# The residual additions of the last stage on VectorE instead of GpSimd, and seven tiles of sums on VectorE instead of five

## The chip, the core and the metric

One core of a Trainium2 chip runs the whole program. The metric is the device time of one execution in microseconds. The engines are called PE (TensorE), DVE (VectorE), ACT (ScalarE), POOL (GpSimd) and SP (SyncE, which here issues transfers and waits).

## What is computed

The reference is one transformer layer with post-normalised branches: attention over 4 x 512 tokens of width 512, then a mixture of 64 experts of which each token uses 8, plus a shared expert.

```python
x = x + _layernorm(_L0_attn_ref(_layernorm(x), Wq, Wk, Wv, Wo))
x = x + _layernorm(_L0_ffn_ref(_layernorm(x), router_w, Wg, Wu, Wd, Wsg, Wsu, Wsd, Wse))

# _L0_ffn_ref: top 8 of 64 experts, weights normalised to sum 1
routed = sum over e of comb[:, e] * ((silu(xt @ wg_e.T) * (xt @ wu_e.T)) @ wd_e.T)
shared = sigmoid(xt @ Wse.T) * ((silu(xt @ Wsg.T) * (xt @ Wsu.T)) @ Wsd.T)
return routed + shared
```

The change touches only the last line of this: the sum `routed + shared`, its layer normalisation, and the addition to `x`.

## The kernel before

The 2048 tokens are 16 tiles of 128 rows (TILES). Attention runs first, then the router and the shared expert, then a loop over some 158 tiles of gathered rows for the experts. Each expert tile's result is added by POOL's indirect DMA into one of three tables in HBM (`sum_rows`, 3 x 2048 x 512, TABLES = 3); the first table starts from the shared expert's output, the others from zero. When the last of these writes has landed, POOL raises `s_routed`, and the last stage begins, written out by hand and without a loop in the machine code.

The last stage, for the 16 tiles in order:

- **SP** waits for `s_routed` and issues 16 loads (L369), 768 KB each: for tile i the three partial sums of its 128 tokens, 128 x 3 x 512, into `sums_of(i)`. These lie in the storage of earlier stages, so the profile calls them `big` (tiles 0 to 7), `x_t` (8 to 11) and `attn_t` (12 to 15). Behind the loads SP issues the 16 outputs (L375), 256 KB each, in order, each once its tile's last addition is done (`s_fin` from POOL, `s_fin_dve` from DVE).
- **PE** sums the three parts of the tiles in `SUM_ON_PE` by three matmuls with the identity matrix into a PSUM bank (L1021); the trace shows each matmul as two instructions. Before, these are tiles 0, 1, 3, 4, 6, 7, 9, 10, 12, 13 and 15. Four banks take turns.
- **DVE** sums the other five tiles (2, 5, 8, 11, 14) by two additions (L1353, L1354). For every tile it takes the statistics (L1359, from PSUM or from SBUF) and aggregates them to mean and variance (L1360). One step later, for tile i - 1, it inverts the deviation (L1364) and forms the bias as a product of mean and inverse (L1365, 128x1). `step(...)` makes the next instruction of DVE wait for the end of this one.
- **ACT** takes the square root for tile i (L695), then normalises tile i - 1 with scale and bias (L700) back into `sums_of(i - 1)[:, 0, :]` and raises `s_norm`.
- **POOL** adds the normalised tile to `x_sb` (L526, the residual) for 14 tiles; DVE does it for tiles 13 and 15 behind all its other work (L1370).

What the engines wait for is set by semaphores: DVE for `s_sums[i]` (a load) or `s_sum_ps` (PE), for `s_lnf` (ACT's square root) before L1364, and for `s_norm` before a residual; ACT for `s_lnb` and `s_lnd` from DVE; PE for `s_sums[i]`, and from its fifth tile on for `s_norm` of the tile that had the bank before.

Of the kernel before, what the change touches and what calls it, by code (L numbers as in the profile page):

```python
# [11 lines left out]
ALU = mybir.AluOpType  # L12
# [9 lines left out]
TILES = B * TB  # L22
# [27 lines left out]
FIRST_STEPS = [("xt", 0), ("xt", 1), ("proj", 0), ("xt", 2), ("proj", 1), ("xt", 3), ("proj", 2), ("qkt", 0),  # L50
               ("proj", 3), ("qkt", 1)]

LAST_ON_DVE = (TILES - 3, TILES - 1)
NOWHERE = TABLES * B * S
SUM_ON_PE = tuple(i for i in range(TILES) if i % 3 != 2)
LAST_ON_POOL = tuple(i for i in range(TILES) if i not in LAST_ON_DVE)

NORM_X_AT = (BLOCKS - 6, BLOCKS - 5, BLOCKS - 3, BLOCKS - 2)

# [1 line left out]
def sandwich_kernel(nc, x, wqkv, wo, router, experts, rope, mask, ident, before, ones, upto, below,  # L61
                    steps, count, token, out):
    ctx = ExitStack()
    with ctx:
        def sb(name, shape, dtype=FP32):
            return ctx.enter_context(nc.sbuf_tensor(name, shape, dtype))

        def sem(name):
            return ctx.enter_context(nc.semaphore(name))


        x_sb = sb("x_sb", [P, TILES, D])
# [88 lines left out]
        def sums_of(i):  # L161
            return sums[i // TB][:, i % TB, :, :]
# [120 lines left out]
        s_lnd = sem("s_lnd")  # L283
        s_norm = sem("s_norm")
        s_fin = sem("s_fin")
        s_fin_dve = sem("s_fin_dve")
        s_out = sem("s_out")
        s_x2d = [sem(f"s_x2d{p}") for p in range(2)]
        s_combd = sem("s_combd")
# [7 lines left out]
        def sum_bank(i):  # L297
            return ps[:, 4 + SUM_ON_PE.index(i) % 4, :]

# [22 lines left out]
        def _(sp):  # L322
# [45 lines left out]
            for i in range(TILES):  # L368
                sp.dma_start(sums_of(i), all_sums_v[:, i, :, :]).then_inc(s_sums[i], 16)  # L369
            for i in range(TILES):  # L370
                if i in LAST_ON_POOL:
                    sp.wait_ge(s_fin, LAST_ON_POOL.index(i) + 1)
                else:
                    sp.wait_ge(s_fin_dve, LAST_ON_DVE.index(i) + 1)
                sp.dma_start(out_v[:, i, :], x_sb[:, i, :]).then_inc(s_out, 16)  # L375
            sp.wait_ge(s_out, 16 * TILES)

# [1 line left out]
        def _(pool):  # L379
# [45 lines left out]
            for i in range(TILES + 4):  # L425
                if i < TILES:
                    pool.wait_ge(s_stat, i + 1)
                    pool.tensor_tensor(out=x_sb[:, i, :], in0=x_sb[:, i, :], in1=delta[:, i % 2, :],
                                       op=ALU.add).then_inc(s_x1, 1)
                if i == 0:  # L430
                    pool.memset(earlier[:, 0, :], 0.0).then_inc(s_first, 1)
                if i >= 4:
                    k = i - 4
# [3 lines left out]
                    else:  # L437
                        pool.wait_ge(s_prefix, k)
                    pool.tensor_tensor(out=earlier[:, k + 1, :], in0=earlier[:, k, :], in1=chosen[:, k, :],
                                       op=ALU.add).then_inc(s_prefix, 1)  # L440

            for i in range(TILES):
                pool.wait_ge(s_up, i + 1)
                if i >= 2:
                    pool.wait_ge(s_sht, i - 1)
                pool.tensor_tensor(out=hidden[:, i % 2, :], in0=gate[:, i % 2, :], in1=up_s[:, i % 2, :],
                                   op=ALU.mult).then_inc(s_shid, 1)
# [72 lines left out]
                pool.wait_ge(s_scatter[p], (full * 2 + (5 if p == 0 else 4)) * 16)  # L520
                pool.sem_inc(s_issue, 1)
            pool.sem_inc(s_routed, 1)

            for i in LAST_ON_POOL:
                pool.wait_ge(s_norm, i + 1)
                pool.tensor_tensor(out=x_sb[:, i, :], in0=x_sb[:, i, :], in1=sums_of(i)[:, 0, :],  # L526
                                   op=ALU.add).then_inc(s_fin, 1)

        @block.scalar
        def _(act):  # L530
# [161 lines left out]
            for i in range(TILES + 1):  # L692
# [3 lines left out]
                if i >= 1:  # L696
                    k = i - 1
                    act.wait_ge(s_lnd, k + 1)
                    total = sum_bank(k) if k in SUM_ON_PE else sums_of(k)[:, 0, :]
                    act.activation(sums_of(k)[:, 0, :], total, ACT.Identity, bias=moments[:, k, 0:1],  # L700
# [3 lines left out]
        def _(pe):  # L704
# [310 lines left out]

            for n, i in enumerate(SUM_ON_PE):
                pe.wait_ge(s_sums[i], 16)
                if n >= 4:
                    pe.wait_ge(s_norm, SUM_ON_PE[n - 4] + 1)
                for p in range(TABLES):  # L1020
# [4 lines left out]
        def _(dve):  # L1025
# [118 lines left out]
            def step(ins):  # L1144

                own[0] += 1
                ins.then_inc(s_own, 1)
                dve.wait_ge(s_own, own[0])
# [7 lines left out]
            for i in range(TILES + 4):  # L1156
                y_in, x_in, l_in = i < TILES, 1 <= i <= TILES, i >= 4
                r, k = i - 1, i - 4
# [73 lines left out]
            for half in range(2):  # L1232
                dve.wait_ge(s_slots_ps, half + 1)
                dve.scalar_tensor_tensor(out=slots[:, 8 * half:8 * half + 8, :],
                                         in0=ps[:, half, :].rearrange("p (t e) -> p t e", e=E), scalar=1.0,
                                         in1=chosen[:, 8 * half:8 * half + 8, :], op0=ALU.add,
# [30 lines left out]
            for m in range(TILES * K):  # L1267
                t, k = divmod(m, K)
# [78 lines left out]
            def total_of(i):  # L1347
                if i in SUM_ON_PE:
                    dve.wait_ge(s_sum_ps, SUM_ON_PE.index(i) + 1)
                    return sum_bank(i)  # L1350
                y = sums_of(i)[:, 0, :]
                dve.wait_ge(s_sums[i], 16)
                step(dve.tensor_tensor(out=y, in0=y, in1=sums_of(i)[:, 1, :], op=ALU.add))  # L1353
                step(dve.tensor_tensor(out=y, in0=y, in1=sums_of(i)[:, 2, :], op=ALU.add))  # L1354
                return y

            for i in range(TILES + 1):
                if i < TILES:
                    step(dve.bn_stats(stats[:, i, :], total_of(i)))  # L1359
                    dve.bn_aggr(moments[:, i, :], stats[:, i, :]).then_inc(s_lnb, 1)  # L1360
                if i >= 1:
                    k = i - 1
                    dve.wait_ge(s_lnf, k + 1)
                    step(dve.reciprocal(rstd[:, k:k + 1], rstd[:, k:k + 1]))  # L1364
                    dve.scalar_tensor_tensor(out=moments[:, k, 0:1], in0=moments[:, k, 0:1], scalar=-1.0,  # L1365
                                             in1=rstd[:, k:k + 1], op0=ALU.mult, op1=ALU.mult).then_inc(s_lnd, 1)

            for i in LAST_ON_DVE:
                dve.wait_ge(s_norm, i + 1)
                dve.tensor_tensor(out=x_sb[:, i, :], in0=x_sb[:, i, :], in1=sums_of(i)[:, 0, :],  # L1370
                                  op=ALU.add).then_inc(s_fin_dve, 1)


def _constants():
# [55 lines left out]
```

## Time and profile before

| | us |
|---|---|
| median of 3 runs | 1173.39 |
| lowest, highest | 1172.31, 1174.42 |
| the profiled execution, in all | 1172.27 |
| its span, first to last instruction | 1170.4 |
| busy PE / DVE / ACT / POOL | 1074.4 / 670.3 / 505.3 / 630.5 |
| first load of the last stage issued | 1115.44 |
| last residual addition ends | 1165.60 |

The profile is of one execution. Times in it count from the first instruction. A row of the timeline gives start, duration, engine, line, operation, the tiles written and read, and in brackets how long the engine had been idle and who released it; several equal instructions in a row are merged. The chain of waits is followed back from the last instruction: at each step to what released it. Matmuls are pipelined and their ends are modelled, and spans on POOL are rough. The granted clock of PE has two levels, 1.00 (2.4 GHz) and 0.50 (1.2 GHz).

### The profile page before, as it was taken

Reading aid. Unit: us, or ns where it says so; the run is one execution under the profiler, and the core shown is the slowest. Engines: PE = TensorE matmul, PEld = TensorE weight load, DVE = VectorE, ACT = ScalarE, POOL = GpSimd, SP = SyncE. Lnnn points to the kernel's source line nnn. Section 1 sums busy time; section 2 is a strip of 40 time slices with the busy share of each in tenths; the row PEclk is TensorE's granted clock in tenths of the full one; section 3 lists DMA queues with packets and bytes.
Section 4 is the critical chain, followed back from the end, with each engine's and each line's share of the span. In section 5 each row is a group of like instructions: output and inputs, shape, how many; then the busy total and the mean of one; then the engine's idle time right before and its main releaser. Section 6 shows DMA issues by size and latency. Waiting matters only on the chain.

```text
span 1170.4 us, 24429 instructions
## 1 busy us (share of the span) xinstructions
PE 1074.4 (92%) x6281; PEld 724.3 (62%) x6282; DVE 670.3 (57%) x2288; ACT 505.3 (43%) x1421; POOL 630.5 (54%) x648
## 2 busy tenths in 40 slices
PE   5999899899999979988869999999999999999973
PEld 3555566555566546555547777777777777677621
DVE  5666566556666668867635544544444444454447
ACT  2666566566666644436622222222222222222223
POOL 3433333433333313321148788887888888788824
PEclk9999999999999999989989999999999999999987
DMA  9700000000000052100169999999999999997796
GB/s 316 288 2 1 3 1 1 2 2 1 1 2 2 1 196 84 63 19 19 66 198 213 219 215 251 236 237 238 256 231 251 243 228 277 258 230 151 114 326 252
DMA packets 66279, 166.73 MB, mean 142 GB/s; under 512 B 15378, under 2 KB 17170, under 8 KB 66080
## 3 DMA queue, kind: packets, MB, share of 16 engines
q0 software_dynamic: 38496, 83.95, 32.5%
q1 hardware_dynamic: 27712, 81.88, 19.9%
q8 instruction: 39, 0.64, 0.2%
q14 instruction: 32, 0.26, 0.1%
HBM read 119.85 MB, written 62.65 MB: 156 GB/s over the span
## 4 chain that ended last, share of the span: by engine, by line
PE 66%; DMA 18%; DVE 6%; issue 5%; ACT 2%; POOL 2%; POOLq 0%; DVEq 0%; SPq 0%; ACTq 0%
PE ps L721 15%; PE ps L982 12%; DMA sum_rows<-x_t,idx 11%; PE ps L780 6%; PE ps L993 6%; DMA x_t<-x_rows,idx 5%; PE ps L838 4%; PE ps L750 4%; PE ps L800 4%; PE ps L966 3%; PE ps L874 2%; PE ps L735 2%; PE ps L890 2%; PE ps L854 1%; POOL x_t L464 1%
## 5 line engine op out<-in xcount | busy, mean ns | idle before, releaser
L982 PE MATMUL ps<-big,work 128*128 x1264 | 300.1, 380 | 0.0
L470 POOL DMA_INDIRECT sum_rows<-x_t,idx x157 | 249.9, 1592 | 53.8 <-issue 40.2
L982 PEld LDWEIGHTS ps<-big,work 128*128 128x128 f32 x1264 | 228.7, 191 | 24.8
L464 POOL DMA_INDIRECT x_t<-x_rows,idx x159 | 166.3, 1046 | 58.9 <-issue 29.0
L721 PE MATMUL ps<-big 128*128 128x384 f32 x512 | 180.1, 495 | 2.1 <-ACT big L539 1.7
L390 POOL TENSOR_TENSOR work<-qkv_all,rope_sb 128x256 f32<-128x256 f32 x64 | 46.8, 731 | 243.6 <-ACT qkv_all L544 243.6
L675 ACT ACTIVATE work<-ps 128x512 f32<-128x512 f32 x159 | 95.0, 597 | 185.4 <-PE ps L966 114.2
L993 PE MATMUL ps<-big,work 128*128 x314 | 160.9, 594 | 0.6 <-issue 0.5
L966 PEld LDWEIGHTS ps<-ident_sb,x_t 128*128 128x128 f32 x636 | 78.3, 142 | 105.9 <-issue 71.9
L1087 DVE CUSTOM_DVE_ANT_0 ps<-ps,mask_sb 128x128 f32<-128x128 f32 (+3 forms) x256 | 120.5, 512 | 24.1 <-PE ps L750 23.4
L563 ACT ACTIVATE work<-ps,neg_max 128x128 f32<-128x128 f32 (+3 forms) x256 | 132.5, 528 | 3.3 <-DVE neg_max L1087 2.2
L721 PEld LDWEIGHTS ps<-big 128*128 128x128 f32 x512 | 94.3, 194 | 56.9 <-issue 4.0
L1311 DVE SCALAR_TENSOR_TENSOR work<-work,small,ps 128x128 f32<-128x128 f32 x157 | 54.5, 347 | 128.5 <-ACT work L680 93.4
L680 ACT ACTIVATE work<-ps 128x128 f32<-128x128 f32 x157 | 43.6, 278 | 195.7 <-PE ps L982 141.8
L569 ACT ACTIVATE x_t<-ps 128x128 f32<-128x128 f32 (+2 forms) x192 | 77.0, 436 | 90.5 <-PE ps L780 90.5
L966 PE MATMUL ps<-ident_sb,x_t 128*128 128x128 f32 x636 | 97.5, 276 | 17.7 <-DMA x_t<-x_rows,idx 15.8
L780 PE MATMUL ps<-ident_sb,work 128*128 128x128 f32 x640 | 98.6, 285 | 9.1 <-issue 6.0
L1319 DVE TENSOR_SCALAR x_t<-ps 128x512 f32<-128x512 f32 x157 | 106.8, 681 | 0.0
L780 PEld LDWEIGHTS ps<-ident_sb,work 128*128 128x128 f32 x640 | 69.0, 142 | 46.1 <-issue 35.1
L1108 DVE TENSOR_TENSOR attn_t<-ps,work 128x128 f32 (+1 forms) x64 | 18.6, 291 | 110.2 <-PE ps L800 110.2
L1305 DVE TENSOR_SCALAR small<-x_t 128x1 f32 x158 | 24.3, 154 | 76.1 <-issue 72.3
L993 PEld LDWEIGHTS ps<-big,work 128*128 128x128 f32 x314 | 59.1, 190 | 10.7 <-issue 3.0
(184 smaller groups left out, 1471.7 us busy)
## 6 DMA issues: line engine op xcount, KB each, us to landing
big<-experts SPq DMA_DIRECT2D x65, 768.0 KB, 14.4
sum_rows<-x_t POOLq DMA_DIRECT2D x4, 2048.0 KB
big<-sum_rows SPq DMA_DIRECT2D x8, 768.0 KB, 9.6
x_rows<-work SPq DMA_DIRECT2D x16, 256.0 KB, 2.0
sum_rows<-attn_t POOLq DMA_DIRECT2D x2, 2048.0 KB
out<-x_sb SPq DMA_DIRECT2D x16, 256.0 KB, 6.1
x_sb<-x SPq DMA_DIRECT2D x3, 1024.0 KB, 10.5
x_t<-sum_rows SPq DMA_DIRECT2D x4, 768.0 KB, 13.1
```

The costliest lines, as they stand in the source:

```text
L464: pool.indirect_dma_start(rows[:, q, :], None, x2_rows, bass.IndirectOffsetOnAxis(ap=idx[:, q, 0:1], axis=0), bounds_check=last_row, oob_i ...
L470: pool.indirect_dma_start(all_sums, bass.IndirectOffsetOnAxis(ap=idx[:, q, 1:2], axis=0), y_sb[:, q, :], None, bounds_check=last_sum, oob_ ...
L563: act.activation(probs[:, h, 0:n], s_bank[h][:, 0:n], ACT.Exp, bias=neg_max[:, h:h + 1], scale=-1.0, accum_out=den[:, h:h + 1]).then_inc(s ...
L569: act.activation(probs_t[:, i % 2, h, 0:qt + 1, :], pt_bank[h % 2].rearrange("p (k n) -> p k n", k=TB)[:, 0:qt + 1, :], ACT.Copy).then_inc ...
L675: act.activation(rows_t[:, p, :, :], ps[:, p, :].rearrange("p (c n) -> p c n", c=DC), ACT.Copy).then_inc(s_xg, 1)
L721: mm = pe.matmul(bank[:, 0:QKV], x_t[:, c, bass.ts(t, P)], wqkv_sb[:, c, g % G, :], start=(c == 0), stop=(c == DC - 1))
L780: mm = pe.transpose(pt_bank[h % 2][:, bass.ts(c, P)], probs[:, h, bass.ts(c, P)], ident_sb[:, :])
L966: mm = pe.transpose(ps[:, p, bass.ts(c, P)], rows[:, q, bass.ts(c, P)], ident_sb[:, :])
L982: mm = pe.matmul(ps[:, 2 + p, 0:GATEUP], rows_t[:, p, c, :], w_ring[:, slot, c * GATEUP:(c + 1) * GATEUP], start=(c == 0), stop=(c == DC - 1))
L993: pe.matmul(ps[:, 5 + p, :], hidden_t[:, p, :], w_ring[:, slot, DC * GATEUP:WCOLS], start=True, stop=True).then_inc(s_dn, 1)
L1087: dve.tensor_tensor_reduce(sc, sc, mask_sb[:, S - n:S], -SCALE, 3.0e38, ALU.add, ALU.min, neg_max[:, h:h + 1]).then_inc(s_masked, 1)
L1319: dve.tensor_scalar(y_sb[:, q, :], ps[:, 5 + q % 2, :], 1.0, None, ALU.mult).then_inc(s_y, 1)
```

## The change

POOL's loop of residual additions goes, with `LAST_ON_POOL`, `LAST_ON_DVE` and `s_fin_dve`. DVE adds the residual of every tile within its loop, three steps behind the statistics, and the loop is two steps longer. `SUM_ON_PE` becomes tiles 1, 2, 4, 6, 7, 9, 11, 12 and 14; DVE sums tiles 0, 3, 5, 8, 10, 13 and 15. SP waits for one semaphore.

```diff
-LAST_ON_DVE = (TILES - 3, TILES - 1)
-SUM_ON_PE = tuple(i for i in range(TILES) if i % 3 != 2)
-LAST_ON_POOL = tuple(i for i in range(TILES) if i not in LAST_ON_DVE)
+SUM_ON_PE = tuple(i for i in range(TILES) if i not in (0, 3, 5, 8, 10, 13, 15))
...
             for i in range(TILES):
-                if i in LAST_ON_POOL:
-                    sp.wait_ge(s_fin, LAST_ON_POOL.index(i) + 1)
-                else:
-                    sp.wait_ge(s_fin_dve, LAST_ON_DVE.index(i) + 1)
+                sp.wait_ge(s_fin, i + 1)
                 sp.dma_start(out_v[:, i, :], x_sb[:, i, :]).then_inc(s_out, 16)
...
-            for i in LAST_ON_POOL:
-                pool.wait_ge(s_norm, i + 1)
-                pool.tensor_tensor(out=x_sb[:, i, :], in0=x_sb[:, i, :], in1=sums_of(i)[:, 0, :],
-                                   op=ALU.add).then_inc(s_fin, 1)
...
-            for i in range(TILES + 1):
+            for i in range(TILES + 3):
                 if i < TILES:
                     step(dve.bn_stats(stats[:, i, :], total_of(i)))
                     dve.bn_aggr(moments[:, i, :], stats[:, i, :]).then_inc(s_lnb, 1)
-                if i >= 1:
+                if 1 <= i <= TILES:
                     k = i - 1
...
-            for i in LAST_ON_DVE:
-                dve.wait_ge(s_norm, i + 1)
-                dve.tensor_tensor(out=x_sb[:, i, :], in0=x_sb[:, i, :], in1=sums_of(i)[:, 0, :],
-                                  op=ALU.add).then_inc(s_fin_dve, 1)
+                if i >= 3:
+                    k = i - 3
+                    dve.wait_ge(s_norm, k + 1)
+                    dve.tensor_tensor(out=x_sb[:, k, :], in0=x_sb[:, k, :], in1=sums_of(k)[:, 0, :],
+                                      op=ALU.add).then_inc(s_fin, 1)
```

How it moves the instructions of DVE. At the start of the last stage, behind the last copy of the expert loop, before:

```order
L1319 TENSOR_SCALAR x_t<-ps 128x512
L1359 BN_STATS stats<-ps 128x6
L1360 BN_AGGR moments<-stats 128x2
L1359 BN_STATS stats<-ps 128x6
L1360 BN_AGGR moments<-stats 128x2
L1364 RECIPROCAL rstd<-rstd 128x1
L1365 SCALAR_TENSOR_TENSOR moments<-moments,rstd 128x1
L1353 TENSOR_TENSOR big<-big 128x512
L1354 TENSOR_TENSOR big<-big 128x512
L1359 BN_STATS stats<-big 128x6
```

and in the changed kernel (where the lines are 11 lower: 1342 and 1343 are the two additions, 1348 and 1349 the statistics, 1353 and 1354 the factors):

```order
L1308 TENSOR_SCALAR x_t<-ps 128x512
L1342 TENSOR_TENSOR big<-big 128x512
L1343 TENSOR_TENSOR big<-big 128x512
L1348 BN_STATS stats<-big 128x6
L1349 BN_AGGR moments<-stats 128x2
L1348 BN_STATS stats<-ps 128x6
L1349 BN_AGGR moments<-stats 128x2
L1353 RECIPROCAL rstd<-rstd 128x1
L1354 SCALAR_TENSOR_TENSOR moments<-moments,rstd 128x1
L1348 BN_STATS stats<-ps 128x6
L1349 BN_AGGR moments<-stats 128x2
```

Tile 0 is now summed by DVE ahead of everything, and the first two tiles that need PE are 1 and 2. At the end of the stage on DVE, before, from the additions of tile 14 on:

```order
L1353 TENSOR_TENSOR attn_t<-attn_t 128x512
L1354 TENSOR_TENSOR attn_t<-attn_t 128x512
L1359 BN_STATS stats<-attn_t 128x6
L1360 BN_AGGR moments<-stats 128x2
L1364 RECIPROCAL rstd<-rstd 128x1
L1365 SCALAR_TENSOR_TENSOR moments<-moments,rstd 128x1
L1359 BN_STATS stats<-ps 128x6
L1360 BN_AGGR moments<-stats 128x2
L1364 RECIPROCAL rstd<-rstd 128x1
L1365 SCALAR_TENSOR_TENSOR moments<-moments,rstd 128x1
L1364 RECIPROCAL rstd<-rstd 128x1
L1365 SCALAR_TENSOR_TENSOR moments<-moments,rstd 128x1
```

and now, from the residual of tile 11 and the additions of tile 15 on:

```order
L1359 TENSOR_TENSOR x_sb<-x_sb,x_t 128x512
L1342 TENSOR_TENSOR attn_t<-attn_t 128x512
L1343 TENSOR_TENSOR attn_t<-attn_t 128x512
L1348 BN_STATS stats<-attn_t 128x6
L1349 BN_AGGR moments<-stats 128x2
L1353 RECIPROCAL rstd<-rstd 128x1
L1354 SCALAR_TENSOR_TENSOR moments<-moments,rstd 128x1
L1359 TENSOR_TENSOR x_sb<-x_sb,attn_t 128x512
L1353 RECIPROCAL rstd<-rstd 128x1
L1354 SCALAR_TENSOR_TENSOR moments<-moments,rstd 128x1
L1359 TENSOR_TENSOR x_sb<-x_sb,attn_t 128x512 x3
```

The residuals (now L1359) stand between the steps, one per tile, and three remain behind the last factors; the two additions of the last tile, 15, are DVE's own. On POOL the last stage's 14 additions are gone and nothing stands in their place:

```order
L513 ISA x2
L520 ISA
L526 TENSOR_TENSOR x_sb<-x_sb,big 128x512 x8
L526 TENSOR_TENSOR x_sb<-x_sb,x_t 128x512 x4
L526 TENSOR_TENSOR x_sb<-x_sb,attn_t 128x512 x2
```

is what POOL had before behind its last indirect DMA; the changed program ends there with the three waiting instructions.

## Rows read from the trace of the kernel before

**Rows 1.** Busy time by stretch; count in brackets; last clock, DMA share, GB/s.
```profile
core 0: us, PE busy (x) PEld busy (x) DVE busy (x) ACT busy (x) POOL busy (x), PEclk, DMA share, GB/s
1120.00:1130.00 10.00, 10.00 (x20) 4.51 (x21) 3.72 (x9) 1.31 (x3) 0.92 (x1) 0.84 1.05 388
...
1140.00:1150.00 10.00, 8.79 (x21) 3.52 (x19) 9.66 (x20) 4.68 (x9) 5.50 (x5) 1.00 1.05 388
```

**Rows 2.** Chain of waits: start, duration, what; its start and end in this stage.
```profile
1115.44 4.50 DMA big<-sum_rows
1119.98 7.02 PE ps L1021 x12
1127.03 0.71 DVE stats L1359
...
1162.42 0.19 DVE moments L1360
```

**Rows 3.** Timeline of DVE: first tiles, POOL still idle (or starting at 1129.08).
```profile
1124.45 0.70 DVE L1359 BATCH_NORM_STATS2 stats<-ps 128x6 f32<-128x512 f32 x1 [13.91 <-PE ps L1021]
...
1127.03 0.70 DVE L1359 BATCH_NORM_STATS2 stats<-ps 128x6 f32<-128x512 f32 x1 [1.66 <-PE ps L1021]
...
1128.10 0.68 DVE L1353 TENSOR_TENSOR big<-big 128x512 f32<-128x512 f32 x1
...
1128.82 0.69 DVE L1354 TENSOR_TENSOR big<-big 128x512 f32<-128x512 f32 x1
...
1130.62 0.69 DVE L1359 BATCH_NORM_STATS2 stats<-ps 128x6 f32<-128x512 f32 x1
```

**Rows 4.** Timeline and groups of instructions: DVE where POOL adds residuals.
```profile
1131.59 1.26 POOL L526 TENSOR_TENSOR x_sb<-x_sb,big 128x512 f32<-128x512 f32 x1 [0.95 <-ACT big L700]
1131.60 1.26 DVE L1365 SCALAR_TENSOR_TENSOR moments<-moments,rstd 128x1 f32<-128x1 f32 x1
...
1133.79 2.95 POOL L526 TENSOR_TENSOR x_sb<-x_sb,big 128x512 f32<-128x512 f32 x2 [0.94 <-ACT big L700]
1133.85 1.77 DVE L1353 TENSOR_TENSOR big<-big 128x512 f32<-128x512 f32 x1
...
L1365 DVE SCALAR_TENSOR_TENSOR moments<-moments,rstd 128x1 f32<-128x1 f32 x16 | 7.0, 434 | 0.6
L1353 DVE TENSOR_TENSOR x_t<-x_t 128x512 f32<-128x512 f32 x2 | 3.5, 1764 | 0.0
L1354 DVE TENSOR_TENSOR x_t<-x_t 128x512 f32<-128x512 f32 x2 | 3.3, 1636 | 0.1
```

**Rows 5.** Issue and time to landing: second and last of the 16 loads.
```profile
1115.88 0.48 SPq L369 DMA_DIRECT2D big<-sum_rows  x1
big<-sum_rows SPq DMA_DIRECT2D x1, 768.0 KB, 6.0
...
1137.53 1.91 SPq L369 DMA_DIRECT2D attn_t<-sum_rows  x1
attn_t<-sum_rows SPq DMA_DIRECT2D x1, 768.0 KB, 13.3
```

**Rows 6.** Busy time by stretch: PE at its start, and with gaps between tiles.
```profile
1122.50:1123.00 0.50, 0.50 (x2) 0.29 (x1) 0.00 (x0) 0.00 (x0) 0.00 (x0) 0.50 1.04 393
1123.00:1123.50 0.50, 0.50 (x2) 0.15 (x2) 0.00 (x0) 0.00 (x0) 0.00 (x0) 0.78 1.07 410
...
1144.00:1146.00 2.00, 1.16 (x3) 0.68 (x4) 1.93 (x4) 0.00 (x0) 0.52 (x1) 1.00 1.05 387
```

**Rows 7.** Timeline and output issues: the end of the kernel.
```profile
1161.70 0.69 DVE L1359 BATCH_NORM_STATS2 stats<-ps 128x6 f32<-128x512 f32 x1
...
1163.24 0.69 DVE L1370 TENSOR_TENSOR x_sb<-x_sb,attn_t 128x512 f32<-128x512 f32 x1
...
1164.40 1.20 DVE L1370 TENSOR_TENSOR x_sb<-x_sb,attn_t 128x512 f32<-128x512 f32 x1 [0.47 <-ACT attn_t L700]
...
out<-x_sb SPq DMA_DIRECT2D x3, 256.0 KB, 2.0
```

**Rows 8.** Timeline of DVE in the expert loop: two instructions without a wait between.
```profile
1103.47 0.68 DVE L1319 TENSOR_SCALAR x_t<-ps 128x512 f32<-128x512 f32 x1
1104.07 0.28 DVE L1323 TENSOR_SCALAR work<-ps 128x128 f32<-128x128 f32 x1
```

More of the change, by code:

```diff
@@ L285, in sandwich_kernel @@
         s_fin = sem("s_fin")
-        s_fin_dve = sem("s_fin_dve")
         s_out = sem("s_out")
```

## Prediction, made before the changed kernel was run

> **What bounds the kernel now.** The diff touches only the end, from the first load of a sums tile on, so I read that stretch alone. The time by stage [rows 1] shows the rate of the loads and how much POOL has to do beside VectorE; the chain of waits [rows 2] shows which engine sets the end. The loads start at 1115.44, the first lands 4.5 us later, TensorE sums two tiles in its slow clock, and from 1127.03 to 1162.6 every piece of the chain is VectorE; TensorE, ScalarE and the DMA queue are never in it again. So the end is VectorE's own instruction stream plus what holds it up.
>
> Clean cycles [rows 3]. A tile summed on TensorE costs VectorE 1.07 us (statistics at 1127.03, next tile's first instruction at 1128.10). A tile that VectorE sums costs 2.52 (1128.10 to 1130.62): two additions 0.72 apart, then the same cycle.
>
> Cycles with POOL at work [rows 4]. At 1131.59 POOL starts a residual; VectorE's 128x1 product, clean 0.16, starts 10 ns later and takes 1.26, ending with POOL's addition. At 1133.85 a 0.68 addition takes 1.77. L1365 sums to 7.0 us over 16 instructions where 16 x 0.16 is 2.6: 4.4 lost. The first statistics at 1124.45 and the last at 1161.70 [rows 7] are 37.25 apart. Ten TensorE tiles (10.7), five own (12.6) and the slower first tile (2.58 for 1.07, so 1.5) make 24.8. That leaves 12.4. The groups account for it: the 4.4, and for four tiles both additions, 1.77 + 1.64 where 1.37 is clean, 4 x 2.04 = 8.2, together 12.6. It is VectorE standing behind POOL.
>
> The Trainium skill has this ("SBUF — State Buffer", Who interferes with whom): a VectorE instruction with two inputs in SBUF and a GpSimd one that reads SBUF cannot run together, the later waits for the whole of the earlier. The rows agree: 1.26 for 0.16. By that page nothing is blocked once POOL is silent, which is the sum below; if it were false here, rival C.
>
> **What the change removes.** POOL's 14 residuals, and the 12.4 us with them. The other cause of long additions would be the loads into the same memory; at 1128.10 to 1129.5 they run at 0.68 and 0.69 while DMA moves 388 GB/s and POOL has done nothing yet [rows 1, 3]. POOL frees nobody else: it is in no wait but SP's for s_fin.
>
> **What it adds on VectorE.** Sixteen residual additions in the stream (two of them stood at its end before), and two more tiles to sum (seven for five). An uncontended residual takes 0.69 [rows 7]. In the stream it is followed by an instruction that waits for nothing of it, so its price is start to start. The nearest rows are a 0.68 tensor_scalar of the same size and its follower 0.60 later [rows 8]. I take 0.61, the same 0.08 less than its duration; the upper end is 0.72, as L1353 to L1354, if the follower had to wait. Nothing lower is plausible.
>
> The skill speaks against my 0.61 ("VectorE: DVE Perf Modes", The DRAIN you can't avoid): eight copies took the same time with a semaphore after each as with one at the end. By that a residual would cost the 0.72, and the end would be 1.6 later (15 x 0.11). The 0.60 of rows 8 decides for me; it is the second half of rival B.
>
> **The start is a new wait.** Tile 0 goes from TensorE to VectorE. VectorE can begin when it lands at 1119.94 and is through its statistics and aggregation at about 1122.3. TensorE now starts with tile 1, which lands at 1115.88 + 6.0 = 1121.88 [rows 5], 1.94 later than tile 0. Before, TensorE's first tile took 4.47 from start to statistics (1119.98 to 1124.45), as the granted clock was 0.50 (the lower level, 1.2 GHz) after the idle stretch; the half microsecond from 1123.0 shows 0.78, so it rose to 1.00 at about 1123.2, 3.2 behind the first matmul [rows 6]; the second took 2.58. With the same warm-up: statistics of tile 1 at 1124.45 + 1.94 = 1126.39, of tile 2 at 1128.97. So VectorE's four-microsecond head start is spent waiting, then 1.5 more on tile 2. Doing tile 0 there costs and gains nothing on the path, since what follows hangs on TensorE.
>
> **The sum**, from the statistics of tile 2 at 1128.97:
> - tile 2: 1.07; tiles 3, 5, 8, 10, 13 on VectorE: 5 x 2.52 = 12.60; tiles 4, 6, 7, 9, 11, 12, 14: 7 x 1.07 = 7.49.
> - the residuals of tiles 0 to 11, one behind each of tiles 3 to 14: 12 x 0.61 = 7.32. Tile 15 begins at 1157.45.
> - its two additions: 1.45. From its statistics: aggregation, the factors of tile 14, residual 12, the factors of 15 and residuals 13, 14, 15. The pieces are 0.72, 0.10, 0.17, 0.07, 0.61, 0.20, 0.07, 0.61, 0.61 and 0.69 = 3.85. ScalarE's square root and both normalisations (0.29 and 0.8 each) fit beside residuals 12 to 14: the last normalisation is through some 2.95 behind the statistics, the last residual starts at 3.16.
> - end of the last residual: 1157.45 + 1.45 + 3.85 = 1162.75, against 1164.40 + 1.20 = 1165.60 now. **2.85 us earlier.**
>
> Are the inputs there? Loads land every 2.07 us ((1137.53 + 13.3 - 1121.88) / 14, rows 5), the last at 1150.8 for a tile that begins at 1157.45; tile 3 lands at 1126.0 and is wanted at 1130.04. TensorE's tile 4 is ready at 1131.55 and wanted at 1133.2, the least slack, 1.6; tile 14 is ready at 1151.5 and wanted at 1155.8. ScalarE has 1.1 us per tile. A residual stands two tiles behind its factors, so it waits for no normalisation until the last. Behind a waiting residual on VectorE would stand the next tile's additions, and behind those ScalarE and SP.
>
> What follows the last addition stays: the last output is issued right behind it and lands in 2.0 [rows 7]. Outputs 12 to 15 come 0.6 to 0.9 apart, 256 KB each, and at 388 GB/s one takes 0.68, so at most 0.1 us of queueing. The profiled execution is 1172.27 us in all (span 1170.4); less 2.85 is 1169.4. It was 1.12 below the median of the three runs, 1173.39; the forecast for a median is **1170.5 us**, 0.24% less. Of this kernel some 0.2% (2.3 us) can be told from no change.
>
> **Rivals.**
> A. As summed, 1170.5, faster. For: the same arithmetic, with the 12.6 from the groups, closes on the stream before within 0.2 us. With the clock rising during tile 1 instead of near its end, 1.0 less, 1169.5.
>
> B. The gain shrinks under 2.3 us. Either TensorE's clock rises later against its first matmul than the 3.2 us of the profile: all of tile 1 at 0.50 is 2 x 2.58 + 0.2 = 5.4 for 4.47, +0.9; tile 2 partly too, +1.7 (before, the same wait would move with it, so part of this cancels against a median). Or each residual costs 0.72, 15 x 0.11 = +1.6. That gives 1171.4 to 1172.2. The untouched 1115 us may also move by what the three runs spread, 2.1.
>
> C. Slower: the long additions are due to the loads after all, not to POOL. Then the 14 sum additions take 1.7 (+1.0 each, 14.0) and the residuals while loads run (about eight) 1.2 (+0.5 each, 4.0), and the end is 18 later than my sum: 1188. It decides as soon as the 30 additions of the stream take 0.10 longer each than clean (3.0, the gain). Against: the clean pair at 388 GB/s and the 10 ns behind POOL at 1131.60.
>
> D. Slower: TensorE, with nine tiles and gaps of 1 to 2 us between them, stays at or falls to 0.50. A tile is then 5.16; nine end at 1121.9 + 46.4 = 1168.3, and 1.07 + 0.61 + 1.45 + 3.85 behind that is 1175.3, 12.5 over my sum: 1183. From a rise about 9 us after the first matmul on (3.2 + 2 x 2.85) the gain is gone. Against: from 1144 to 1146 TensorE was busy for 58% and the clock stayed 1.00 [rows 6], and in a slow clock the backlog fills the gaps.
>
> E. The gain stays in the queue: the last outputs come faster than they can be written. Were three of them in the queue when the last residual ends, that is 3 x 0.68 = 2.0 more, 1172.5. Against: SP issues outputs from 1139.5 on, behind the last load; by then my sum has residuals 0 to 2 done, and from there they come 1.7 to 3.1 apart.
>
> **Chances.** A 0.58, B and E 0.36 (same), C 0.03, D 0.03 (slower). Faster 0.58, same 0.36, slower 0.06. The range takes in A's early clock with 1.3 of spread (1168.2), and E or B's worst with 0.7 to 1.0 of it (1173.2).
>
> **What would show it.** In the profile after: L1354 (the product) at 0.16 everywhere and both sum additions at 0.68 to 0.69; 16 residuals at 0.69 with 0.61 to the next start; statistics of tile 2 near 4.5 + 2.6 behind TensorE's start; the chain VectorE alone from there for 33.8 us; POOL without busy time. A median above 1173, an addition over 0.8 with POOL idle, or VectorE waiting for TensorE after tile 2 would make the prediction wrong.

## The result, and the profile after

The changed kernel is faster: 1167.32 us median of six runs (1166.20 to 1169.17) against 1173.76 for the kernel before in the same runs, a ratio of 0.9948 (95% interval 0.9936 to 0.9961), 6.4 us. The profiled execution took 1166.61 (span 1164.8) against 1172.27 (span 1170.4), 5.7 us less. The forecast was 2.85 us less and a range that ended at 1168.2: right in its sign, and the size was half of what came. In another set of runs the ratio is 0.9943 (0.9922 to 0.9965), so the gain is not chance.

Where the time went in the two profiles, measured from the issue of the stage's first load:

| us | before | after | forecast for after |
|---|---|---|---|
| first load issued, in the span | 1115.44 | 1115.18 | 1115.44 |
| TensorE's first tile starts | 4.54 behind it | 6.41 | 6.48 |
| statistics of tile 2 | 14.11 | 13.37 | 13.53 |
| last residual ends | 50.16 | 46.97 | 47.31 |
| end of the span behind the last residual | 4.8 | 2.65 | 4.8 |

The last three lines are the case. The stage up to the last residual came as forecast within 0.34 us: 3.2 less where 2.85 was worked out. The rest, 2.15, is behind the last residual, where the prediction said nothing would change. Another 0.26 of the 5.6 between the two spans is the expert loop ahead of the stage.

VectorE's timeline after, at the start and around tiles 2 and 3 (columns as in rows 3; L1342 and L1343 are the two additions, L1348 and L1349 the statistics, L1353 and L1354 the factors, L1359 the residual):

```profile
1119.57 0.69 DVE L1342 TENSOR_TENSOR big<-big 128x512 f32<-128x512 f32 x1 [8.32 <-DMA big<-sum_rows]
...
1125.97 0.70 DVE L1348 BATCH_NORM_STATS2 stats<-ps 128x6 f32<-128x512 f32 x1 [4.04 <-PE ps L1010]
...
1128.55 0.70 DVE L1348 BATCH_NORM_STATS2 stats<-ps 128x6 f32<-128x512 f32 x1 [1.42 <-PE ps L1010]
...
1129.62 0.69 DVE L1342 TENSOR_TENSOR big<-big 128x512 f32<-128x512 f32 x1
...
1132.14 0.68 DVE L1359 TENSOR_TENSOR x_sb<-x_sb,big 128x512 f32<-128x512 f32 x1
1132.74 0.69 DVE L1348 BATCH_NORM_STATS2 stats<-ps 128x6 f32<-128x512 f32 x1
```

Both waits of the prediction are there, 4.04 for tile 1 and 1.42 for tile 2. From 1128.55 on VectorE waits for nobody. A tile of its own costs 2.52 (1129.62 to 1132.14), a residual 0.60 from start to start (1132.14 to 1132.74). The groups of instructions of VectorE in the stage, which answer to [rows 4] (busy time, mean ns, idle time before):

```profile
L1359 DVE TENSOR_TENSOR x_sb<-x_sb,big 128x512 f32<-128x512 f32 x8 | 5.5, 684 | 0.0
...
L1354 DVE SCALAR_TENSOR_TENSOR moments<-moments,rstd 128x1 f32<-128x1 f32 x16 | 2.5, 159 | 0.6
...
L1343 DVE TENSOR_TENSOR x_t<-x_t 128x512 f32<-128x512 f32 x2 | 1.4, 692 | 0.1
...
L1342 DVE TENSOR_TENSOR x_t<-x_t 128x512 f32<-128x512 f32 x2 | 1.4, 684 | 0.0
```

The product is at 159 ns in the mean for 434, the additions at 684 and 692 for 1764 and 1636.

Now the end. What SyncE waited for in the last microseconds, before and then after (who waited for whom: us, times, longest; L64 and L62 are the end of the program):

```profile
SPq L375 <- POOL x_sb L526: 7.5, 4, 3.5
...
SPq L64 <- PEq L64: 2.4, 1, 2.4
SPq L64 <- DMA out<-x_sb: 1.8, 1, 1.8
```

```profile
SPq L62 <- DMA out<-x_sb: 1.9, 1, 1.9
SPq L62 <- PEq L62: 0.2, 1, 0.2
```

The last output took 1.8 or 1.9 in both. Behind it SyncE waited another 2.4 us before and 0.2 after, for the other engines to reach the end. The row names PE, which had finished long ago (its last instruction, a DRAIN, starts at 1150.9 and takes 2.9; here every engine has one as its last instruction but for the final semaphores). The instructions on the program's last line say who was late. Before (duration min/median/max in ns, then the start):

```profile
L64 POOLq EVENT_SEMAPHORE  x2: 17/17/17, 1170.3 to 1170.3; - x2
L64 PEldq DRAIN  x1: 2878/2878/2878, 1150.9 to 1150.9; - x1
L64 ACTq DRAIN  x1: 1034/1034/1034, 1163.4 to 1163.4; - x1
L64 POOLq DRAIN  x1: 6469/6469/6469, 1163.7 to 1163.7; - x1
```

After:

```profile
L62 POOLq EVENT_SEMAPHORE  x2: 17/17/17, 1164.6 to 1164.7; - x2
L62 POOLq DRAIN  x1: 5134/5134/5134, 1115.2 to 1115.2; - x1
```

GpSimd ends the program with a DRAIN as every engine does, and after the change its one takes 5134 ns with nothing left to do. Before, it starts with GpSimd's last residual (1163.77, 1.27 us), which ends at 1165.04, and it ends 5.1 behind that, at 1170.2. The span ends there, at 1170.4; the last residual of all, VectorE's, ended at 1165.6, and the difference is the 4.8 that the prediction carried over. After, it runs from 1115.2 to 1120.3, beside the first load, and costs nothing.

### The profile page after: what moved, and what is told of

Same layout as the page of the kernel before. It is cut to its first block, busy times and chain, and to the rows that moved or that the text cites. A ratio compares the mean times of both kernels' runs of the same rounds, so it can differ in the third digit from the quotient of the medians.

```text
span 1164.8 us, 24407 instructions
## 1 busy us (share of the span) xinstructions
PE 1068.5 (92%) x6269; PEld 721.7 (62%) x6270; DVE 668.9 (57%) x2306; ACT 505.4 (43%) x1421; POOL 610.8 (52%) x634
## 4 chain that ended last, share of the span: by engine, by line
PE 74%; DMA 12%; DVE 6%; issue 4%; ACT 2%; POOL 1%; DVEq 0%; SPq 0%; POOLq 0%; ACTq 0%
PE ps L971 16%; PE ps L710 15%; PE ps L982 8%; PE ps L769 7%; DMA sum_rows<-x_t,idx 6%; DMA x_t<-x_rows,idx 5%; PE ps L827 4%; PE ps L955 4%; PE ps L739 4%; PE ps L789 4%; PE ps L863 2%; PE ps L724 2%; PE ps L879 2%; PE ps L843 1%; PE ps L977 1%
```

## The experiments

The theory after the result has two parts: VectorE's stream (as predicted) and GpSimd's 5.13 us behind its last instruction. Its rivals are: the end of the span behind the last residual is output and nothing else; GpSimd hinders VectorE through what both wait for and not through SBUF; the new choice of tiles carries the gain. All stage times below are from one profile each. The ratios are to the kernel before, in the same set of runs, with their 95% intervals.

| kernel | first load | clock rises behind TensorE's first tile | last residual behind first load | span end behind last residual | ratio (95%) |
|---|---|---|---|---|---|
| before | 1115.44 | 3.2 | 50.16 | 4.8 | 1 |
| changed | 1115.18 | 3.1 | 46.97 | 2.65 | 0.9948 (0.9936 to 0.9961) |
| changed, again | 1114.75 | 3.3 | 47.44 | 2.6 | 0.9943 (0.9922 to 0.9965) |
| tiny memset | 1115.22 | 5.6 | 48.45 | 4.5 | 0.9983 (0.9969 to 0.9996) |
| tiny memset, again | 1112.99 | 2.9 | 46.98 | 4.5 | 0.9970 (0.9958 to 0.9982) |
| five sums | 1115.64 | 3.7 | 44.81 | 2.65 | 0.9941 (0.9926 to 0.9956) |
| GpSimd ends early | 1117.21 | 4.8 | 50.18 | 2.7 | 0.9974 (0.9960 to 0.9987) |
| seven sums, GpSimd adds | 1115.51 | 5.4 | 50.57 | 4.8 | 1.0002 (0.9992 to 1.0011) |
| GpSimd reads | 1116.37 | 5.8 | 53.20 | 2.6 | one run |
| GpSimd writes | 1116.31 | 4.2 | 47.46 | 2.6 | one run |
| eleven idle matmuls | 1112.62 | fell to 0.50 at 1119.5 | 47.08 | 2.6 | 0.9947 (0.9930 to 0.9963) |
| thirteen idle matmuls | 1117.52 | 1.00 all along | 45.37 | 2.6 | 0.9948 (0.9930 to 0.9966) |
| four sums | 1114.28 | 4.2 | 43.73 | 2.6 | 0.9919 (0.9902 to 0.9937) |
| four sums, idle matmuls | 1114.82 | 1.00 all along | 43.63 | 2.65 | 0.9927 (0.9907 to 0.9948) |

The first column is why the ratios are blunter than the stage: in the profiles the expert loop ahead of it ends anywhere from 1112.6 to 1117.5, whatever the kernel, and that spread is as large as the effects.

**GpSimd's last instruction.** The changed kernel with one tiny instruction more:

```diff
             pool.sem_inc(s_routed, 1)
+            pool.wait_ge(s_norm, TILES)
+            pool.memset(mark_sb[:, :], 0.0)
```

`mark_sb` is a new tile of 128 x 1 that nobody uses.

> The changed kernel plus one tiny GpSimd instruction: a memset of a spare 128x1 tile once the last normalisation is done. Theory (drain): after a GpSimd instruction that instruction stream needs 5.13 us (its DRAIN, 5134 ns in the changed kernel) before the kernel may end; put behind the last normalisation at about 1161.2 that reaches 1166.5, where the changed kernel ended at 1164.8, so the span grows by about 2.0 us and the ratio to before is 0.9965 instead of 0.9948. VectorE's last residual stays at 47.0 us behind the first load. Rival (port only): GpSimd costs only by holding VectorE up; a 128x1 memset holds up nothing, the ratio stays 0.9948 within 0.3 us.

Its timeline and the DRAIN of its GpSimd, in the first profile:

```profile
1162.77 0.10 POOL L519 MEMSET mark_sb<- 128x1 f32 x1 [49.68 <-ACT attn_t L692]
...
L62 POOLq DRAIN  x1: 5259/5259/5259, 1162.7 to 1162.7; - x1
```

An instruction of 0.10 us, which nobody waits for, has 5.1 us behind it and ends the span at 1168.2, 4.5 behind the last residual instead of 2.65. The theory's 2.0 us are there, 1.9. The ratio came out higher than expected, 0.9983 for 0.9965, some 2.1 us; in the profile the last residual is 1.5 us later than in the changed kernel, with a late rise of TensorE's clock. The same kernel in a second set of runs:

> The changed kernel plus the tiny GpSimd memset once more. The first time its ratio was 0.9983 (0.9969 to 0.9996) where 0.9965 was expected, and its profile showed 1.9 us behind the last residual and 1.5 us for a late rise of TensorE's clock. Theory (the drain alone is systematic, the clock's moment is chance): span end 4.4 to 4.6 us behind the last residual again, clock rise anywhere from 3 to 5.6 us behind TensorE's first matmul, ratio 0.9965 within 0.0012. Rival (the added instruction costs more than its drain, by something not seen): 0.998 or more again.

The second profile has the early rise (last residual at 46.98, as in the changed kernel), the same 5259 ns, the span end 4.5 behind the last residual; the ratio is 0.9970 (0.9958 to 0.9982). In both profiles the span ends 1.9 later behind the last residual than in the changed kernel, which is the drain; the other difference of the first profile goes with the clock. That the ratio of the first set of nine runs lay 0.0013, or 1.5 us, above that of the second is not explained: each set has one profile.

**GpSimd earlier.** The kernel before, with `LAST_ON_DVE` from two tiles to four:

```diff
-LAST_ON_DVE = (TILES - 3, TILES - 1)
+LAST_ON_DVE = (TILES - 4, TILES - 3, TILES - 2, TILES - 1)
```

> The kernel before with the residuals of tiles 12 to 15 on VectorE at the end of its stream, so GpSimd's last addition is tile 11's, about 7 us before the end. Theory (drain): its 5.13 us are then over before the last output; the span ends 2.7 us behind the last residual instead of 4.8. VectorE ends about 0.8 us earlier (1165.6 to 1164.8), since two additions of GpSimd less hold it up and two residuals more stand at the end. Together 2.9 us less: 0.9975. Rival (the 4.8 us are output and end of program): only the 0.8, 0.9993.

```profile
1159.71 1.27 POOL L526 TENSOR_TENSOR x_sb<-x_sb,x_t 128x512 f32<-128x512 f32 x1 [0.94 <-ACT x_t L700]
...
L64 POOLq DRAIN  x1: 6466/6466/6466, 1159.7 to 1159.7; - x1
```

The DRAIN ends at 1166.2, before the last residual (1167.39), and the span ends 2.7 behind that. This is the drain's part of the gain with nothing else of the change. VectorE's 0.8 does not show in the whole stage (50.18 for 50.16), as the clock rose 4.8 instead of 3.2 behind TensorE's first matmul and the statistics of the second tile came 12.38 behind the first load instead of 11.59. From there to the last residual it is 37.80 for 38.57, the expected 0.8. The ratio is 0.9974 for an expected 0.9975.

**The two halves of the change apart.** GpSimd's residuals with the new tiles, and VectorE's residuals with the old tiles:

> The kernel before with the new choice of tiles alone (VectorE sums 0, 3, 5, 8, 10, 13, 15), GpSimd adds the residuals as before. Theory: VectorE's stream gets 2 x 1.45 more and about two more additions held up by GpSimd, so it ends 2 to 3 us later than before; GpSimd's last addition also later, and the span ends some 4.8 behind it: 1.002 of the kernel before. Rival (the new choice of tiles carries a part of the gain): 0.998 or less.

> The changed kernel with the old choice of tiles summed on VectorE (2, 5, 8, 11, 14). Theory (VectorE's stream sets the end): two tiles fewer cost VectorE 2 x 1.45 less, and the first tile is again TensorE's; by the same arithmetic as in the prediction the last residual ends 44.7 to 45.0 us behind the first load where the changed kernel has 47.0. The last outputs then come near the rate of the queue, so 2.1 to 2.4 us less in all: ratio 0.993. Rival (seven sums are needed, TensorE would be late with eleven tiles): TensorE's last tile is wanted at about 41 behind the first load and is ready at 38; if it is later than that, the time is the same as the changed kernel or above, 0.995.

Seven sums with GpSimd adding are no slower than before, 1.0002; the expected 2 to 3 us did not come, the stage grew by 0.4. Two more sums are 2.9 us of VectorE, but less of its work met GpSimd:

```profile
L1365 DVE SCALAR_TENSOR_TENSOR moments<-moments,rstd 128x1 f32<-128x1 f32 x16 | 8.1, 503 | 0.6
...
L1353 DVE TENSOR_TENSOR x_t<-x_t 128x512 f32<-128x512 f32 x2 | 2.4, 1224 | 0.0
...
L1354 DVE TENSOR_TENSOR big<-big 128x512 f32<-128x512 f32 x3 | 2.1, 692 | 0.1
```

The product loses 5.5 (8.1 less 2.6); of the seven tiles only two have their additions held up (a mean of 1224 over two tiles, one of them clean, and the same in `attn_t`), 4.0 in all. That is 9.5 for 12.6 before, which pays for the two sums. The 0.4 of the stage goes with the clock: it rose 5.4 behind TensorE's first matmul, and the statistics of tile 2 came 14.56 behind the first load for 13.37 in the changed kernel. By this estimate the new choice alone might save 0.8 with an early clock; in the ratio of ten runs it is worth nothing either way.

With VectorE adding and five sums the last residual ends 44.81 behind the first load, in the expected 44.7 to 45.0 and 2.16 sooner than in the changed kernel. TensorE is not late: its last tile is done at 1150.97 + 2.84, VectorE takes its statistics at 1156.62. So in these profiles the seven sums are a cost of the change, but not as the two additions of two more tiles (2 x 1.45), as was expected. 1.78 of the 2.16 is the start: the statistics of TensorE's second tile come 11.59 behind the first load for 13.37, since its first tile can begin with the first load, and VectorE's own additions on tile 0 fall into a wait. The other 0.38 is one more tile summed on VectorE for two on TensorE behind that (2.52 less 2 x 1.07). The residuals on VectorE alone would have taken 5.3 us off the stage (50.16 to 44.81). The ratio, 0.9941 where 0.993 was expected, can't be told from the changed kernel's, so in the time of the whole kernel this cost is not shown.

**How GpSimd holds VectorE up.** The changed kernel with thirteen idle instructions on GpSimd, in the storage of the mask, which nobody needs any more; once additions (reading and writing SBUF), once memsets (writing only):

```diff
             pool.sem_inc(s_routed, 1)
+            pool.memset(mask_sb[:, :], 0.0).then_inc(s_idle, 1)
+            for i in range(TILES - 3):
+                pool.wait_ge(s_norm, i + 1)
+                pool.wait_ge(s_idle, i + 1)
+                pool.tensor_tensor(out=mask_sb[:, :], in0=mask_sb[:, :], in1=mask_sb[:, :], op=ALU.add).then_inc(s_idle, 1)
```

> The changed kernel plus thirteen idle GpSimd additions of 128x512, each once the normalisation of tiles 0 to 12 is done, on a spare tile that nobody else uses (read and written in SBUF, the mask's storage). Nothing depends on them. Theory (an instruction of GpSimd that reads SBUF keeps VectorE's instructions with two SBUF inputs out, and nothing else connects them): additions and products on VectorE take up to 1.26 longer again, some 0.8 to 1.0 us lost per GpSimd addition, so the last residual ends 57 to 60 us behind the first load instead of 47. Rival (the hold-up in the kernel before came from both engines waiting for the same data and semaphores): 47.

> The same with thirteen memsets of the same 128x512 spare tile in place of the additions: GpSimd writes SBUF and reads nothing. Theory (it is the read side): VectorE's additions stay at 0.69 and the last residual at 47 us (46.6 to 48.5 with the clock's rise) behind the first load; GpSimd is through some 7 us before the end, so its 5.13 us are hidden too. Rival (any GpSimd access to SBUF): 50 or more.

Groups on VectorE with the additions (L1349 is the second addition, L1360 the product), then the timeline at one of them:

```profile
L1360 DVE SCALAR_TENSOR_TENSOR moments<-moments,rstd 128x1 f32<-128x1 f32 x16 | 4.6, 285 | 0.6
L1349 DVE TENSOR_TENSOR x_t<-x_t 128x512 f32<-128x512 f32 x2 | 2.8, 1411 | 0.1
...
1137.63 1.17 POOL L522 TENSOR_TENSOR mask_sb<-mask_sb 128x512 f32<-128x512 f32 x1 [0.94 <-ACT big L695]
1137.94 1.41 DVE L1349 TENSOR_TENSOR big<-big 128x512 f32<-128x512 f32 x1
```

The same with the memsets (L1359 the product, L1348 the second addition):

```profile
L1359 DVE SCALAR_TENSOR_TENSOR moments<-moments,rstd 128x1 f32<-128x1 f32 x16 | 2.5, 159 | 0.6
...
L1348 DVE TENSOR_TENSOR x_t<-x_t 128x512 f32<-128x512 f32 x2 | 1.4, 691 | 0.1
...
1136.49 0.53 POOL L520 MEMSET mask_sb<- 128x512 f32 x1 [1.18 <-ACT big L694]
1136.76 0.69 DVE L1348 TENSOR_TENSOR big<-big 128x512 f32<-128x512 f32 x1
```

Nothing waits for these instructions and they touch no data of anybody, yet with additions on GpSimd VectorE's two-input instructions are held up, and with memsets every one is at its clean length. The comparison rests on the second additions: four of them start while GpSimd is at work in either kernel, and take 1.41 beside an addition and 0.69 beside a memset. A memset, 0.53 us long for 1.04 of an addition, is over 0.01 to 0.05 us before VectorE's next product starts, so for the product this experiment leaves open whether writing would hold it up. A shared wait is excluded for both, as both kernels wait for the same semaphore at the same place. So it is GpSimd's reading of SBUF. The Trainium skill says the same ("SBUF — State Buffer", Who interferes with whom): a VectorE instruction with two SBUF inputs contends with a GpSimd instruction that reads SBUF, and not with one that only writes it. The size was not as expected: 53.20 for 57 to 60. Seven products lost 2.0 and four second additions 2.9, 4.9 in all; another 1.35 is the start, with the clock's late rise (statistics of tile 2 14.72 behind the first load, 13.37 in the changed kernel). These additions take 1.03 to 1.33, most of them less than the residuals' 1.26, and fall beside products and second additions only: VectorE's residuals, at 680 to 686, were never held up.

**The clock at the start.** The changed kernel, idle matmuls in a free PSUM bank ahead of TensorE's first sums tile:

```diff
+            for _ in range(11):
+                pe.matmul(ps[:, 7, :], ident_sb[:, :], mask_sb[:, :], start=True, stop=True)
             for n, i in enumerate(SUM_ON_PE):
                 pe.wait_ge(s_sums[i], 16)
```

> The changed kernel plus eleven idle matmuls of 128x512 on TensorE between the expert loop's last one and the first sums tile, about 9.4 us of work in an unused bank, results not used. Theory (the start of the stage hangs on TensorE's first tile in its slow clock): the clock stays at 1.00, the first tile takes 2.8 us from start to statistics instead of 4.4, so the last residual ends at 45.4 us behind the first load, 1.6 earlier than in the changed kernel's profile, and always so: ratio to before 0.993. Rival (another wait comes behind it, a load or the outputs): no more than 0.3 less, 0.9945.

The expected 45.4 did not come: the last residual ends 47.08 behind the first load. Busy time by stretch (columns as in rows 1) and the timeline of TensorE in that kernel:

```profile
1116.00:1117.00 1.00, 0.70 (x2) 0.00 (x0) 0.08 (x1) 0.00 (x0) 0.00 (x0) 1.00 1.04 393
1117.00:1118.00 1.00, 0.00 (x0) 0.00 (x0) 0.96 (x2) 0.00 (x0) 0.00 (x0) 1.00 1.08 401
...
1119.00:1120.00 1.00, 1.00 (x2) 0.50 (x3) 0.25 (x2) 0.29 (x1) 0.00 (x0) 0.78 1.04 406
1120.00:1121.00 1.00, 1.00 (x2) 0.34 (x1) 0.00 (x0) 0.00 (x0) 0.00 (x0) 0.50 1.04 397
```

```profile
1107.10 9.61 PE L1006 MATMUL ps<-mask_sb,ident_sb 128*128 128x512 f32 x22
1118.95 5.40 PE L1013 MATMUL ps<-big,ident_sb 128*128 128x512 f32 x8 [2.25 <-DMA big<-sum_rows]
```

The idle matmuls kept the clock at 1.00 and ended 2.25 us before tile 1 came; 0.6 us into the tile the clock fell, and TensorE did most of it at 0.50. So this kernel does not test what it was made for. The next one has thirteen idle matmuls in place of eleven:

> As the kernel with eleven idle matmuls, now with thirteen, 11.1 us of work: in that run TensorE had been idle for 2.25 us when the first tile came and the clock fell to 0.50 during that tile. Theory (the stage's start hangs on the clock in TensorE's first tile): with the gap under 1 us the clock stays at 1.00, statistics of tile 1 come 2.8 us behind TensorE's start, and the last residual ends 45.2 to 45.5 us behind the first load where the changed kernel has 46.97. Span end behind it 2.65 as before. Rival (something else is late next): 46.5 or more although the clock is 1.00.

```profile
1123.84 5.42 PE L1013 MATMUL ps<-big,ident_sb 128*128 128x512 f32 x12 [0.33 <-DMA big<-sum_rows]
...
1126.72 0.70 DVE L1351 BATCH_NORM_STATS2 stats<-ps 128x6 f32<-128x512 f32 x1 [2.53 <-PE ps L1013]
```

With a gap of 0.33 the clock is 1.00 throughout, statistics come 2.9 behind TensorE's start, and the last residual ends at 45.37. The stage hangs on TensorE's first tile: 1.6 us, as expected. The time over the whole kernel does not show it (0.9948 again). In this profile the loop ended late, at 1117.5, where the loop of the kernel with eleven ended at 1112.6; whether the spread is chance or the idle matmuls' doing is open.

**A version that goes on from here.** Four tiles on VectorE, then with idle matmuls:

```diff
-SUM_ON_PE = tuple(i for i in range(TILES) if i not in (0, 3, 5, 8, 10, 13, 15))
+SUM_ON_PE = tuple(i for i in range(TILES) if i not in (2, 5, 8, 12))
```

> The changed kernel with four tiles summed on VectorE (2, 5, 8, 12), twelve on TensorE. Theory (from here the output queue sets the end): VectorE's last residual ends 43.3 to 43.8 us behind the first load, 1.0 to 1.5 earlier than with five (44.8), but the sixteen outputs of 256 KB need 10.8 us behind the last load's landing at 35.5 at the rate seen, so the span ends 47 us behind the first load, 0.3 to 0.5 less than with five. Rival (VectorE's stream still sets it): 1.0 to 1.5 less than with five, 46.2.

> Four tiles on VectorE (2, 5, 8, 12) and eleven idle matmuls ahead of the first sums tile. Theory (with twelve tiles TensorE's rate and the loads set the pace, VectorE has slack early on): only 0.2 to 0.5 us less than with four tiles alone (last residual 43.2 to 43.5 behind the first load, span 46.0), but the late rises of the clock, up to 1.5 us, cannot happen: ratio 0.9915. Rival (the idle matmuls slow the end of the expert loop or the loads): 0.993 or more.

With four sums the last residual ends at 43.73, as expected, but the span ends 46.3 behind the first load, where the queue theory had 47. It ended 2.6 behind the last residual, as wherever GpSimd's DRAIN is over by then, so the output queue did not set it, and the rival is right (46.2). At 0.9919 (0.9902 to 0.9937) it is the fastest kernel of the study, its interval touching the changed kernel's first one at the edge and overlapping the second (0.9922 to 0.9965). The idle matmuls add nothing to it, although the clock is 1.00 from the start: 43.63, where 43.2 to 43.5 was expected. VectorE now waits for TensorE before three tiles in the middle and at the end (0.81, 0.34 and 0.46), and TensorE in turn for loads (0.67 to 0.98), so the loads and the twelve tiles on TensorE set the pace. The last of these waits:

```profile
1154.61 0.70 DVE L1351 BATCH_NORM_STATS2 stats<-ps 128x6 f32<-128x512 f32 x1 [0.46 <-PE ps L1013]
```

The ratio, 0.9927 (0.9907 to 0.9948), was expected at 0.9915, with 0.993 or more for a harmful effect of the idle matmuls; it does not decide between the two.

**The changed kernel again**, beside these:

> The changed kernel itself once more, beside the others on one chip. Theory (its stage time spreads with the moment at which the clock rises behind TensorE's first matmul, 3.0 to 5.6 us in the profiles so far): last residual 47 to 48.5 us behind the first load, span end 2.65 behind it, ratio 0.9948 within 0.0015. Rival (the gain of the first measurement was in part the chip or the day): 0.9965 or more, near the forecast's 0.9976.

The ratio is 0.9943 and the last residual ends at 47.44, as expected. The gain is the kernel's.

## Why the prediction was wrong

**Right, by its own steps.** VectorE bounds the stage: from the statistics of tile 2 on the chain is VectorE alone. The hold-up behind GpSimd was read off rightly as 12.4 to 12.6 us and is gone completely; the product is at 0.16, the additions at 0.68 and 0.69. The residual costs 0.60 from start to start, forecast 0.61. The Trainium skill's measurement that was weighed against it ("VectorE: DVE Perf Modes", The DRAIN you can't avoid), eight copies as long with a semaphore after each as with one at the end, would have made it 0.72, and the trace does not agree. The same section says that a next operation that is not held starts earlier, and that is what the 0.60 shows. The new wait for TensorE's first tile is there with its two parts. Behind tile 2 VectorE never waited for a load, for a bank or for ScalarE. The last residual came 3.19 earlier behind the first load, forecast 2.85: 0.16 because TensorE's start and first two tiles were that much sooner against the load, and the rest for the most part 15 residuals at 0.01 less each. One reading was loose: the second addition of the clean pair in the prediction (1128.82 to 1129.51) was not free of GpSimd, whose first residual starts at 1129.08 [rows 3]; VectorE's had started first and kept its 0.69, and GpSimd's took 1.55 for 1.26.

**Wrong: one sentence.** "What follows the last addition stays." The 4.8 us between the last residual and the end of the span were taken as output and program end and carried over. The output accounts for 2.0 of landing and some 0.7 around it; that is the 2.6 to 2.7 of every kernel whose GpSimd is through early. The 2.15 above it was GpSimd's DRAIN, behind a last residual on GpSimd that ended at 1165.04. The change takes the last instruction off GpSimd and so takes the 2.15 away. 2.85 + 2.15 makes 5.0, and with 0.34 in the stage and 0.26 ahead of it the 5.6 of the two spans. The median came 3.2 below the forecast 1170.5: 2.15, 0.34 and 0.26 make 2.75, and 0.4 came because the profiled execution lay 0.7 below its median after, where the forecast had carried over 1.12. The prediction listed what each engine does in the stage and asked for GpSimd only whether anyone waits for it; its answer, "in no wait but SP's for s_fin", left out the one wait that all engines share, the end of the program.

It could have been read. The waits of SyncE in the kernel before have a row of 2.4 us at the program's last line, after the output had landed, with a releaser that had been done for more than 16 us. Where a row names an engine that was finished long ago, the wait was for another, and the instructions on that line name it. 4.8 us against a landing of 2.0 in the same group of rows [rows 7] was the other sign.

**Of the rivals.** A's mechanism is what happened. B's late clock is real and of the size given: in the profiles the rise comes 2.9 to 5.8 us behind the first matmul of TensorE's first tile, and at 5.6 the last residual is 1.5 later (48.45), in kernels with and without GpSimd's additions alike. That it therefore widens the runs and does not move the ratio is argued from these profiles and not shown. B's dear residual, C (loads lengthen additions), D (the clock stays low) and E (outputs queue) did not occur; E was tried harder with four sums and did not occur there either.

**The range** left out what it had not priced: the bound of the term "end of the kernel" was set at one point, with 0.1 of queueing on it, where its two pieces, 2.0 known and 2.8 unexplained, would have given the term a lower end of 2.0 and the range one 2.8 lower, at 1165.4, and the measured 1167.32 would have been in it.

## What to carry to other kernels

When a time is carried over unchanged, take it apart as well: what of the 4.8 us is a transfer, what is an instruction, and which engine reaches the program's last line last. In this kernel GpSimd needs 5.1 us behind its last instruction, however small that is, so its work should end at least 2.5 us before the last output is issued (5.1 less the 2.65 behind it), and moving its last two residuals, as in the kernel in which GpSimd ends early, is enough.

Look at what GpSimd's help costs the engine that it helps: fourteen residuals of 0.60 each on VectorE (8.4 us) had been moved off it at a price of 12.6 us in its two-input instructions. And when a change does two things, run each alone: here the second half, the new choice of tiles with two more sums, was worth nothing with GpSimd adding and cost 2.2 us of the stage, in one profile of each, with VectorE adding.

## What the runs showed of the hardware

- GpSimd's DRAIN on the program's last line took 5134 ns in the changed kernel, five-sums, idle-matmul and memset kernels alike, 5259 behind a 0.10 memset that had just started, 6232 behind an addition of 1.04, and 6466 to 6506 behind one of 1.27 to 1.31: each time 5.1 to 5.2 us from the end of its last instruction. Those of ScalarE (0.8 to 1.0), VectorE (1.0 to 1.4) and TensorE (2.8 to 4.0, with its last matmuls in it) are shorter. In the changed kernel 1.5 us lay between GpSimd's last DMA instruction and the DRAIN, in the one with memsets 0.2 between the last memset and the DRAIN, and both took 5134; so it does not look like a rest of the work ahead of it. What GpSimd does in these 5.1 us no run shows.
- Thirteen GpSimd additions on a tile of its own, nobody waiting, held eleven of VectorE's two-input instructions up, by 4.9 us in all. Thirteen memsets of the same tile held up none, four of them beside a two-input addition.
- TensorE's granted clock of 1.00 lasted through 2.25 us without matmuls and then fell to 0.50, 0.6 us after they had begun again; after gaps of 0.33 and 0.98 it stayed.
- From a clock of 0.50, the rise to 1.00 came 2.9 to 5.8 us behind the first matmul of the stage, in eleven profiles.
